# GpSimd adds the two tables' sums between the layers of a graph network, TensorE turns one sum

## The chip, the cores and the metric

The kernel runs on one core of a Trainium2 chip. The metric is the time of one execution in microseconds of the device. Engines are written as in the profile: PE is TensorE's matmul, PEld its weight load, DVE is VectorE, ACT is ScalarE, POOL is GpSimd, SP is SyncE, whose queue issues most transfers here.

## The reference

A graph of 6250 nodes with 256 features and 100000 edges, sorted by `dst`, goes through two layers. Layer 0 computes a message for each edge, sums the messages per node, and passes sum and node through a gated unit. Layer 1 is an attention over the edges with 8 heads. Each layer ends in a residual and a layer norm.

```python
msg = relu(concat[h[row], h[col], edge_attr] @ W1.T + b1) @ W2.T + b2
agg = segment_sum(msg, row, N)
gx = agg @ W_ih.T + b_ih                  # xr, xz, xn = split(gx)
gh = h @ W_hh.T + b_hh                    # hr, hz, hn = split(gh)
r, z = sigmoid(xr + hr), sigmoid(xz + hz)
n = tanh(xn + r * hn)
x1 = layernorm(h + (1 - z) * n + z * h)
# layer 1: s_u = x1 @ W_u.T + b_u, s_v = x1 @ W_v.T; softmax over the edges of a node,
# weighted sum of x1[src]; then layernorm(x1 + sum)
```

The kernel moves W2 behind the sum: layer 0 leaves for each node the sum of the 256 hidden values and a count of its edges, and the product of W2 and W_ih (`WcT`) is applied once per node.

## The kernel before

The program runs in phases with a barrier between them: setup, layer 0 over the edges (2/3 of the time), the nodes between the layers (`nodes_phase`), layer 1 over the edges, output. Nodes are dealt with in 49 blocks of 128 (a node in each partition).

Layer 0 adds its sums into two tables in memory, `S0` and `S1`, by turns. The sums of a node are therefore the sum of its rows in both. `nodes_phase` is the stage between the layers, and the only one that the change touches. A step of a block is a small function, and `pipeline(engine, stages)` writes each engine's order by hand: in round `j` an engine runs its steps in the order listed, each for the block that is so many blocks behind as the number beside it says. The first 7 rounds are written out, the rest is a loop with 7 rounds in its body. Steps of a block, in the order of the data:

- SP, `load` (L1318 to L1322): two transfers for `sums[:, 0, j]` and `sums[:, 1, j]`, one each for `hidden` (the products of W_hh) and `xs`. There are buffers for 7 blocks. In the loop a load stands behind `mixed` of the block that held the buffer, and behind the store of the block before that one (L1326), which waits for that block's last step.
- DVE `start` (L1438 to L1442): the count and the two `addend` operations.
- PE `turn_sums` (L1375): four matmuls against the identity, of 128x128 each, turn and add the two sums in PSUM (`psT`), two for each half of the 256 columns. ACT copies `psT` to `sumsT` (L1410).
- PE `gates` (L1385): four matmuls. DVE `keep_gates` (L1448, L1449), ACT sigmoid (L1414), DVE `candidate` (L1454, L1456), ACT tanh (L1418).
- POOL `mix` (L1352, L1353): `xs - cand` and `xs + cand`. DVE `update` (L1461 to L1468): three operations on the mixed values and the moments.
- POOL `deviation` (L1358 to L1363): root and shift of the norm from the moments. ACT normalises (L1424), PE turns `x1` (L1393) and computes the scores (L1400), DVE `finish` (L1473, L1474).

In a round POOL runs `deviation` three blocks behind and then `mix` two blocks behind. DVE runs `candidate` (2), `start` (0), `finish` (6), `keep_gates` (1), `update` (2). PE runs `gates` (1), `turn_sums` (0), `turn_x1` (4), `scores` (5). Each queue is strictly in this order, so POOL's `mix` of a block stands behind its `deviation` of the block before, and that one waits for DVE's `update` of the block before.

Of the kernel before, what the change touches and what calls it, by code (L numbers as in the profile page):

```python
# [7 lines left out]
ALU = mybir.AluOpType  # L8
# [3 lines left out]
P = 128  # L12
N, E, H, ED, NH = 6250, 100000, 256, 64, 8
# [13 lines left out]
NTAB = 2  # L27
# [31 lines left out]
def nth(i, j):  # L59

    return i * UNR + (j + 1)


def pipeline(engine, stages):

    def one_pass(i, first):
        for j in range(UNR):
            for behind, stage in stages:  # L70
                if j >= behind:
                    stage(i, j - behind)
                elif not first:
                    stage(i - 1, UNR + j - behind)

    one_pass(0, True)
    with engine.Fori(1, NI) as i:
        one_pass(i, False)
    for j in range(UNR, UNR + max(behind for behind, _ in stages)):
        for behind, stage in stages:  # L80
            if 0 <= j - behind < UNR:
                stage(NI - 1, j - behind)
# [1192 lines left out]
def nodes_phase(nc, K, D, A):  # L1275
# [3 lines left out]
    with ExitStack() as st:  # L1279
        m = Mem(nc, st, "nd_")  # L1280
        sums = m.sb("sums", [P, NTAB, UNR, UW])
# [15 lines left out]
        psT = m.ps("psT", [P, 512])  # L1297
# [3 lines left out]
        psS = m.ps("psS", [P, 512])  # L1301
        loaded = [m.sem(f"loaded{j}") for j in range(UNR)]
        stored = [m.sem(f"stored{j}") for j in range(UNR)]
        counted, sums_turned, sumsT_ready = m.sem("counted"), m.sem("sums_turned"), m.sem("sumsT_ready")
        gates_done, gates_kept, gates_open = m.sem("gates_done"), m.sem("gates_kept"), m.sem("gates_open")
        cand_ready, cand_done, mixed = m.sem("cand_ready"), m.sem("cand_done"), m.sem("mixed")
# [9 lines left out]
        @block.sync  # L1316
        def _(sp):
            def load(row, j, count=P):  # L1318
                for t in range(NTAB):
                    sp.dma_start(sums[:, t, j, :], D[f"S{t}"][bass.ds(row, P), :]).then_inc(loaded[j], 16)  # L1320
                sp.dma_start(hidden[:, j, :], D["GH"][bass.ds(row, P), :]).then_inc(loaded[j], 16)
                sp.dma_start(xs[0:count, j, :], A["x"][bass.ds(row, count), :]).then_inc(loaded[j], 16)  # L1322

            def store(i, j):
                sp.wait_ge(rows_ready, nth(i, j))
                sp.dma_start(D["X1"][bass.ds(i * (UNR * P) + j * P, P), :], x1[:, j, :]).then_inc(stored[j], 16)  # L1326

            for j in range(UNR):
                load(j * P, j)
            with sp.Fori(0, NI - 2) as i:  # L1330
                for j in range(UNR):

                    sp.wait_ge(mixed, i * (2 * UNR) + 2 * (j + 1))
                    sp.sem_inc(sp_waited, 1)
                    load(i * (UNR * P) + (UNR + j) * P, j)
                    store(i, j)
            for j in range(UNR):
                sp.wait_ge(mixed, (NI - 2) * 2 * UNR + 2 * (j + 1))
                row = (NI - 1) * UNR * P + j * P
                load(row, j, min(P, N - row))  # L1340
                store(NI - 2, j)
            for j in range(UNR):
                store(NI - 1, j)
            for j in range(UNR):
                sp.wait_ge(stored[j], 16 * NI)

        @block.gpsimd
        def _(pool):
            def mix(i, j):

                pool.wait_ge(cand_done, nth(i, j))
                nc.gpsimd.tensor_tensor(tmp[:, j, :], xs[:, j, :], cand[:, j, :], ALU.subtract).then_inc(mixed, 1)  # L1352
                nc.gpsimd.tensor_tensor(y[:, j, :], xs[:, j, :], cand[:, j, :], ALU.add).then_inc(mixed, 1)  # L1353

            def deviation(i, j):

                pool.wait_ge(moments_ready, nth(i, j))
                nc.gpsimd.tensor_tensor(rstd[:, j, :], moments[:, j, 1:2], K["eps"][:, :], ALU.add).then_inc(var_ready, 1)  # L1358
                pool.wait_ge(var_ready, i * (3 * UNR) + (3 * j + 1))
                nc.gpsimd.tensor_tensor(rstd[:, j, :], rstd[:, j, :], K["neghalf"][:, :], ALU.pow).then_inc(var_ready, 1)  # L1360
                nc.gpsimd.tensor_scalar(shift[:, j, :], moments[:, j, 0:1], -1.0, None, ALU.mult).then_inc(var_ready, 1)
                pool.wait_ge(var_ready, i * (3 * UNR) + (3 * j + 3))
                nc.gpsimd.tensor_tensor(shift[:, j, :], shift[:, j, :], rstd[:, j, :], ALU.mult).then_inc(rstd_ready, 1)  # L1363

            pipeline(pool, [(3, deviation), (2, mix)])

        @block.tensor
        def _(pe):
            def turn_sums(i, j):

                pe.wait_ge(sumsT_ready, i * UNR + j)
                pe.wait_ge(loaded[j], i * (16 * (NTAB + 2)) + 16 * (NTAB + 2))
                for k in range(HC):
                    for t in range(NTAB):
                        last = nc.tensor.matmul(psT[:, k * P:(k + 1) * P], sums[:, t, j, k * P:(k + 1) * P], K["ident"][:, :],  # L1375
                                                start=(t == 0), stop=(t == NTAB - 1))
                last.then_inc(sums_turned, 1)

            def gates(i, j):

                pe.wait_ge(gates_kept, i * UNR + max(j - 1, 0))
                pe.wait_ge(sumsT_ready, nth(i, j))
                for target, cols in ((psRZ[j % 2][:, :], slice(0, 2 * H)), (psN[j % 2][:, 0:H], slice(2 * H, 3 * H))):
                    for k in range(HC):
                        t = nc.tensor.matmul(target, sumsT[:, j, k * P:(k + 1) * P], K["WcT"][:, k, cols],  # L1385
                                             start=(k == 0), stop=(k == HC - 1))
                t.then_inc(gates_done, 1)

            def turn_x1(i, j):
                pe.wait_ge(x1T_ready, i * UNR + j)  # L1390
                pe.wait_ge(x1_ready, nth(i, j))
                for k in range(HC):
                    t = nc.tensor.transpose(psX[:, k * P:(k + 1) * P], x1[:, j, k * P:(k + 1) * P], K["ident"][:, :])  # L1393
                t.then_inc(x1_turned, 1)

            def scores(i, j):
                pe.wait_ge(rows_ready, i * UNR + j)
                pe.wait_ge(x1T_ready, nth(i, j))
                for k in range(HC):
                    t = nc.tensor.matmul(psS[:, 0:2 * NH], x1T[:, j, k * P:(k + 1) * P], K["WuvT"][:, k, :],  # L1400
                                         start=(k == 0), stop=(k == HC - 1))
                t.then_inc(scores_done, 1)

            pipeline(pe, [(1, gates), (0, turn_sums), (4, turn_x1), (5, scores)])

        @block.scalar
# [549 lines left out]
def build(nc, x, src, dst, edge_attr, W1, b1, W2, b2, W_ih, b_ih, W_hh, b_hh, W_u, b_u, W_v, out, stop=99):  # L1956
# [15 lines left out]
    with ExitStack() as st:  # L1972
# [19 lines left out]
        if stop < 2:  # L1992
            return
        nodes_phase(nc, K, D, A)
        inner.close()
        if stop < 3:
# [25 lines left out]
```

## Time and profile before

| | us |
|---|---|
| median of 3 runs | 4522.47 |
| lowest and highest | 4519.23, 4522.68 |
| the profiled execution, its own time | 4518.8 |
| its span, first to last instruction | 4517.1 |
| PE busy over the span | 3121.0 (69%) |
| DVE busy | 2158.0 (48%) |
| POOL busy | 3433.0 (76%) |
| ACT busy | 940.8 (21%) |
| first and last record of L1375 in the node phase | 2822.5, 3073.4 |

The node phase runs from about 2818 us to about 3089 us of the span, 6% of it. The shares over the whole span say nothing on it, so the rows further down are taken from its own window. A start in a row is counted from the span's beginning. The records of one engine may overlap by some hundredths of a microsecond, since an instruction's record begins while the one ahead of it ends.

### The profile page before, as it was taken

What the parts mean: (1) busy time and instruction counts of PE and PEld (TensorE: products, weight loads), DVE (VectorE), ACT (ScalarE), POOL (GpSimd) and SP (SyncE); (2) the same over time, 40 slices, a digit from 0 to 9 for tenths busy, and PEclk for the clock granted to TensorE, in tenths of its full rate; (3) what the DMA queues carried; (4) which work ended last, traced back from release to release, by engine and by line L of the source; (5) the groups of instructions that cost most, each with busy time, mean ns of one, the idle gap of its engine ahead of it and who ended that gap; (6) DMA issues with size and microseconds to landing.
All of it is one profiled execution on the core that took longest, in us unless ns stands there. A gap on an engine that the chain in (4) does not pass through costs nothing. (4 is left out here: it accounts for less than half of the span.)

```text
span 4517.1 us, 64322 instructions
## 1 busy us (share of the span) xinstructions
PE 3121.0 (69%) x13560; PEld 1920.1 (43%) x13561; DVE 2158.0 (48%) x4919; ACT 940.8 (21%) x2901; POOL 3433.0 (76%) x2886
## 2 busy tenths in 40 slices
PE   6688787787877878878788875884554554555552
PEld 3354444444444444444444443563433333333331
DVE  6433333333333333333333332886766666666767
ACT  2322222222222222222222221442000000000002
POOL 5568888888888888888888876566777777777775
PEclk8888888888888888888888888996776776776775
DMA  7787776777677767777777775555443344343342
GB/s 227 269 186 128 128 130 130 134 127 130 127 129 130 134 130 130 128 129 129 134 130 130 131 133 92 170 179 169 118 116 115 110 117 115 110 118 115 108 118 74
DMA packets 532854, 604.83 MB, mean 134 GB/s; under 512 B 170317, under 2 KB 451301, under 8 KB 532816
## 3 DMA queue, kind: packets, MB, share of 16 engines
q0 software_dynamic: 198144, 339.26, 39.2%
q1 hardware_dynamic: 319838, 242.37, 19.6%
q10 hardware_dynamic: 14834, 22.79, 1.5%
q8 instruction: 12, 0.20, 0.0%
q14 instruction: 26, 0.21, 0.0%
HBM read 435.31 MB, written 168.84 MB: 134 GB/s over the span
## 5 line engine op out<-in xcount | busy, mean ns | idle before, releaser
L1081 POOL DMA_INDIRECT S<-l_msum,l_sink x784 | 1278.3, 1631 | 279.0 <-issue 208.2
L1606 POOL DMA_INDIRECT l_feats<-X_rows,l_gsrc x880 | 1036.8, 1178 | 297.3 <-issue 258.7
L1064 POOL DMA_INDIRECT l_ga<-A_rows,l_gsrc x784 | 801.3, 1022 | 265.2 <-issue 158.9
L1154 PE MATMUL l_psU<-l_hid,l_same 128*128 128x257 f32 x1568 | 599.9, 469 | 489.7 <-ACT l_hid L1190 487.0
L1127 PE MATMUL l_psC<-l_table,l_onehot 128*128 x4728 | 741.3, 299 | 0.0
L1194 ACT COPY l_msum<-l_psU 128x257 f32<-128x257 f32 x784 | 292.6, 373 | 1877.4 <-POOLq L1080 1450.2
L1672 PE MATMUL l_psU<-l_feats,l_same 128*128 128x264 f32 x1760 | 537.6, 466 | 152.1 <-DVE l_feats L1841 135.2
L1120 PE MATMUL l_psC<-W1cT,l_attrT 64*128 64x256 f32 x1576 | 627.4, 482 | 12.9 <-DMA l_table<-B_rows 12.9
L1127 PEld LDWEIGHTS l_psC<-l_table,l_onehot 128*128 128x128 bf16 x4728 | 429.9, 105 | 373.8 <-issue 307.8
L1154 PEld LDWEIGHTS l_psU<-l_hid,l_same 128*128 128x128 f32 x1568 | 275.1, 220 | 618.3 <-ACT l_hid L1190 602.6
L1672 PEld LDWEIGHTS l_psU<-l_feats,l_same 128*128 128x128 f32 x1760 | 395.4, 233 | 287.5 <-issue 204.4
L1268 DVE TENSOR_TENSOR l_hidden<-l_psG,bgate 128x256 f32<-128x256 f32 x147 | 62.4, 425 | 864.7 <-PE l_psG L1169 864.7
L1120 PEld LDWEIGHTS l_psC<-W1cT,l_attrT 64*128 64x128 f32 x1576 | 264.1, 209 | 270.4 <-issue 237.9
L1226 DVE TENSOR_SCALAR l_togo<-srcT,spare 128x8 f32 x98 | 28.3, 289 | 699.2 <-POOLq L1080 699.2
L1190 ACT ACTIVATE l_hid<-l_ga 128x256 f32<-128x256 f32 x784 | 330.6, 422 | 0.0
L1243 DVE TENSOR_TENSOR l_ga<-l_ga,l_psC 128x256 f32<-128x256 f32 x784 | 308.4, 415 | 40.7 <-PE l_psC L1127 16.7
L1751 DVE TENSOR_TENSOR acc<-acc,l_psU 128x264 f32 x440 | 188.2, 428 | 226.8 <-PE l_psU L1672 194.4
L1841 DVE TENSOR_TENSOR l_feats<-l_feats 128x1024 f32<-128x1024 f32 x220 | 263.9, 1220 | 4.0 <-ACT l_feats L1704 0.4
L1169 PE MATMUL l_psG<-WhhT,l_xgT 128*128 128x256 f32 x588 | 210.8, 446 | 0.0
L1702 ACT ACTIVATE l_shrink<-l_psE 128x8 f32<-128x8 f32 x55 | 9.7, 177 | 954.6 <-PE l_psE L1659 954.6
L1217 DVE TENSOR_TENSOR l_same<-l_srcb,srcT 128x1024 f32<-128x1024 f32 x99 | 121.1, 1224 | 123.9 <-PE l_psU L1154 123.9
L1169 PEld LDWEIGHTS l_psG<-WhhT,l_xgT 128*128 128x128 f32 x588 | 136.8, 233 | 27.5
(357 smaller groups left out, 3264.9 us busy)
## 6 DMA issues: line engine op xcount, KB each, us to landing
l_srcb<-src_rows SPq DMA_DIRECT2D x396, 128.0 KB
l_locb<-lo_rows SPq DMA_DIRECT2D x55, 512.0 KB, 4.0
l_locb<-loc_rows SPq DMA_DIRECT2D x396, 64.0 KB
l_attr<-in_edge_attr SPq DMA_DIRECT2D x197, 128.0 KB, 3.5
GH_rows<-l_hidden SPq DMA_DIRECT2D x49, 384.0 KB
nd_hidden<-GH_rows SPq DMA_DIRECT2D x49, 384.0 KB, 3.1
l_feats<-X_rows,l_gsrc POOLq DMA_INDIRECT x880
S<-su_zeros ACTq DMA_DIRECT2D x12, 1156.5 KB
```

What stands on the lines that cost most here:

```text
L1064: pool.indirect_dma_start(ga[:, s, :], None, D["A"], bass.IndirectOffsetOnAxis(ap=gsrc[h][:, j % HALF:j % HALF + 1], axis=0)).then_inc(gat ...
L1081: pool.indirect_dma_start(D[f"S{j % NTAB}"], bass.IndirectOffsetOnAxis(ap=sink[j // HALF][:, j % HALF:j % HALF + 1], axis=0), msum[:, j % ...
L1120: nc.tensor.matmul(pc(j), attrT[j // 4 % 2][side, j % 4 // 2 * P:(j % 4 // 2 + 1) * P], K["W1cT"][side, :], start=True, stop=False)
L1127: t = nc.tensor.matmul(pc(j), onehot[j // HALF % 2][:, w, j % HALF, :], flat(table[:, bass.ds(blocks[j % 4] + w, 1), n * H:(n + 1) * H]), ...
L1154: nc.tensor.matmul(psU[j % 2][:, 0:UW], same[j // HALF][:, j % HALF, :], hid[:, j % RING, :], start=True, stop=True).then_inc(agg_done, 1)
L1169: t = nc.tensor.matmul(psG[:, 0:H], xgT[:, k * P:(k + 1) * P], K["WhhT"][:, k, n * H:(n + 1) * H], start=(k == 0), stop=(k == HC - 1))
L1190: nc.scalar.activation(hid[:, j % RING, 0:H], ga[:, j % SLOTS, :], ACT.Relu).then_inc(hid_ready, 1)
L1194: nc.scalar.copy(msum[:, j % RING, :], psU[j % 2][:, 0:UW]).then_inc(msum_ready, 1)
L1243: nc.vector.tensor_tensor(ga[:, s, :], ga[:, s, :], pc(j), ALU.add).then_inc(pre_ready, 1)
L1606: pool.indirect_dma_start(feats[r][:, t, :], None, D["X1"], bass.IndirectOffsetOnAxis(ap=gsrc[r][:, t:t + 1], axis=0)).then_inc(gathered[r ...
L1672: i = nc.tensor.matmul(psU[n % 4][:, 0:XW], same[:, t, :], feats[r][:, t, :], start=(t % PAIR == 0), stop=(t % PAIR == PAIR - 1))
L1841: nc.vector.tensor_tensor(f3, f3, w3, ALU.mult).then_inc(weighted, 1)
```

## The change

POOL gets a step `add_pair`: it waits for the block's four transfers and adds the second table's sums to the first's in place, over 256 columns. PE waits for this in place of the transfers, and turns the one sum with two transposes, where four matmuls stood. `add_pair` of the round's own block stands first in POOL's round, ahead of `deviation` and `mix`. The count (column 256) is still added on DVE. A new semaphore, `pair_added`, is taken ahead of those that follow it.

```diff
@@ nodes_phase
+        pair_added = m.sem("pair_added")
...
-            pipeline(pool, [(3, deviation), (2, mix)])
+            def add_pair(i, j):
+                pool.wait_ge(loaded[j], i * (16 * (NTAB + 2)) + 16 * (NTAB + 2))
+                nc.gpsimd.tensor_tensor(sums[:, 0, j, 0:H], sums[:, 0, j, 0:H], sums[:, 1, j, 0:H], ALU.add).then_inc(pair_added, 1)
+
+            pipeline(pool, [(0, add_pair), (3, deviation), (2, mix)])
...
             def turn_sums(i, j):
 
                 pe.wait_ge(sumsT_ready, i * UNR + j)
-                pe.wait_ge(loaded[j], i * (16 * (NTAB + 2)) + 16 * (NTAB + 2))
+                pe.wait_ge(pair_added, nth(i, j))
                 for k in range(HC):
-                    for t in range(NTAB):
-                        last = nc.tensor.matmul(psT[:, k * P:(k + 1) * P], sums[:, t, j, k * P:(k + 1) * P], K["ident"][:, :],
-                                                start=(t == 0), stop=(t == NTAB - 1))
+                    last = nc.tensor.transpose(psT[:, k * P:(k + 1) * P], sums[:, 0, j, k * P:(k + 1) * P], K["ident"][:, :])
                 last.then_inc(sums_turned, 1)
```

On POOL, in the body of the loop, this stands in a row before (the round's end and the next one; the names in brackets are those of semaphores, some of which carry the name that the same number had in the setup phase):

```order
L1352 TENSOR_TENSOR nd_tmp<-nd_xs,nd_cand 128x256 [waits nd_cand_done]
L1353 TENSOR_TENSOR nd_y<-nd_xs,nd_cand 128x256
L1358 TENSOR_TENSOR nd_rstd<-nd_moments,eps 128x1 [waits su_x_out]
L1359 REGISTER_ALU
L1360 TENSOR_TENSOR nd_rstd<-nd_rstd,neghalf 128x1 [waits su_x_keys_ready]
L1361 TENSOR_SCALAR nd_shift<-nd_moments 128x1
```

And with the change, where lines are moved by up to 7:

```order
L1353 TENSOR_TENSOR nd_tmp<-nd_xs,nd_cand 128x256 [waits nd_cand_done]
L1354 TENSOR_TENSOR nd_y<-nd_xs,nd_cand 128x256
L1368 TENSOR_TENSOR nd_sums<-nd_sums 128x256 [waits nd_loaded1]
L1359 TENSOR_TENSOR nd_rstd<-nd_moments,eps 128x1 [waits su_x_keys_ready]
L1360 REGISTER_ALU
L1361 TENSOR_TENSOR nd_rstd<-nd_rstd,neghalf 128x1 [waits su_x_mapped]
L1362 TENSOR_SCALAR nd_shift<-nd_moments 128x1
```

The add of the next round's block stands directly behind the second operation of `mix`, with no other instruction between them.

On PE, in the sixth of the rounds that are written out, before:

```order
L1375 MATMUL nd_psT<-ident,nd_sums 128x128 [waits nd_loaded5,nd_sumsT_ready]
L1375 MATMUL nd_psT<-ident,nd_sums 128x128 x3
L1393 MATMUL nd_psX<-ident,nd_x 128x128 [waits nd_x1_ready,nd_x1T_ready]
L1393 MATMUL nd_psX<-ident,nd_x 128x128
L1400 MATMUL nd_psS<-WuvT,nd_x1T 128x16 [waits nd_x1T_ready,nd_rows_ready]
L1400 MATMUL nd_psS<-WuvT,nd_x1T 128x16
```

And with the change, where the step has two instructions and waits for POOL:

```order
L1379 MATMUL nd_psT<-ident,nd_sums 128x128 [waits nd_pair_added,nd_sumsT_ready]
L1379 MATMUL nd_psT<-ident,nd_sums 128x128
L1396 MATMUL nd_psX<-ident,nd_x 128x128 [waits nd_x1_ready,nd_x1T_ready]
L1396 MATMUL nd_psX<-ident,nd_x 128x128
```

What stands around it on PE is as before.

## Rows read from the trace of the kernel before

**Rows 1.** Busy time in a stretch: length, PE, PEld, DVE, ACT, POOL, clock, DMA.

```profile
2900.00:2920.00 20.00, 17.71 (x89) 12.43 (x88) 17.38 (x52) 8.57 (x20) 12.78 (x24) 1.00 0.60 183
```

**Rows 2.** Waits of DVE and PE from 2867 to 3024: total us, times, longest.

```profile
DVE nd_tmp L1461 <- POOL nd_y L1353: 10.4, 29, 0.5
PE nd_psS L1400 <- DVE nd_x L1474: 19.9, 25, 1.1
```

**Rows 3.** Timeline, POOL and DVE in one round: start, us, engine, line, idle before.

```profile
2901.11 0.28 POOL L1358 TENSOR_TENSOR nd_rstd<-nd_moments,eps 128x1 f32<-128x1 f32 x1 [1.79 <-DVE nd_moments L1468]
...
2902.57 0.48 DVE L1442 SCALAR_TENSOR_TENSOR nd_addend<-b2ih,nd_count,bgate 128x256 f32<-128x256 f32 x1
...
2902.83 0.27 POOL L1363 TENSOR_TENSOR nd_shift<-nd_shift,nd_rstd 128x1 f32<-128x1 f32 x1
...
2903.06 0.73 POOL L1352 TENSOR_TENSOR nd_tmp<-nd_xs,nd_cand 128x256 f32<-128x256 f32 x1
...
2903.74 0.73 POOL L1353 TENSOR_TENSOR nd_y<-nd_xs,nd_cand 128x256 f32<-128x256 f32 x1
...
2904.50 0.42 DVE L1461 TENSOR_TENSOR nd_tmp<-nd_tmp,nd_rz 128x256 f32<-128x256 f32 x1 [0.37 <-POOL nd_y L1353]
...
2904.96 0.42 DVE L1463 TENSOR_TENSOR nd_y<-nd_y,nd_tmp 128x256 f32<-128x256 f32 x1
...
2905.42 0.43 DVE L1465 BATCH_NORM_STATS2 nd_stats<-nd_y 128x6 f32<-128x256 f32 x1
...
2905.99 0.18 DVE L1468 BATCH_NORM_AGGREGATE nd_moments<-nd_stats 128x2 f32<-128x6 f32 x1 [0.15 <-DVE nd_stats L1465]
...
2906.26 0.28 POOL L1358 TENSOR_TENSOR nd_rstd<-nd_moments,eps 128x1 f32<-128x1 f32 x1 [1.79 <-DVE nd_moments L1468]
```

**Rows 4.** Timeline, PE in one round, and SP's last load in the same round.

```profile
2903.72 1.96 PE L1385 MATMUL nd_psRZ<-WcT,nd_sumsT 128*128 128x512 f32 x4
...
2905.59 0.33 SPq L1322 DMA_DIRECT2D nd_xs<-in_x  x1
...
2906.39 1.05 PE L1375 MATMUL nd_psT<-ident,nd_sums 128*128 128x128 f32 x8
...
2907.28 0.38 PE L1393 MATMUL nd_psX<-ident,nd_x 128*128 128x128 f32 x2
...
2908.40 0.62 PE L1400 MATMUL nd_psS<-WuvT,nd_x1T 128*128 128x16 f32 x4 [0.74 <-DVE nd_x L1474]
```

**Rows 5.** Transfers into the `sums` buffers, from the view of that tile.

```profile
DMA to landing us min/median/max: 1.9/2.1/4.8
```

**Rows 6.** Timeline at the phase's start: DVE and POOL side by side.

```profile
2834.43 0.75 DVE L1440 SCALAR_TENSOR_TENSOR nd_addend<-b2ih,nd_count,nd_hidden 128x512 f32<-128x512 f32 x1
2834.86 0.91 POOL L1352 TENSOR_TENSOR nd_tmp<-nd_xs,nd_cand 128x256 f32<-128x256 f32 x1 [25.85 <-ACT nd_cand L1418]
2835.10 0.95 DVE L1442 SCALAR_TENSOR_TENSOR nd_addend<-b2ih,nd_count,bgate 128x256 f32<-128x256 f32 x1
...
2835.74 0.90 POOL L1353 TENSOR_TENSOR nd_y<-nd_xs,nd_cand 128x256 f32<-128x256 f32 x1
```

**Rows 7.** Timeline in the output phase: a large POOL add, a DVE operation on 3 columns.

```profile
4460.45 3.95 POOL L1904 TENSOR_TENSOR x_rows<-acc,x_rows 128x1792 f32<-128x1792 f32 x1
4461.06 3.36 DVE L1932 SCALAR_TENSOR_TENSOR ot_shift<-ot_moments,ot_rstd 128x3 f32<-128x3 f32 x1
```

**Rows 8.** Timeline at the phase's start: the first block on PE.

```profile
2822.50 2.04 PE L1375 MATMUL nd_psT<-ident,nd_sums 128*128 128x128 f32 x8 [30.48 <-DMA nd_xs<-in_x]
```

**Rows 9.** Stretches where the clock fell (columns as in Rows 1), and two rounds around them.

```profile
2970.20:2973.60 3.40, 2.27 (x7) 1.24 (x8) 2.96 (x10) 1.49 (x4) 1.81 (x3) 0.91 0.35 105
2973.60:2977.00 3.40, 3.40 (x13) 2.47 (x12) 2.69 (x9) 0.42 (x1) 3.04 (x6) 0.58 0.61 176
```

**Rows 10.** Timeline: POOL's first instruction of a round, two rounds apart.

```profile
2968.36 0.19 POOL L1358 TENSOR_TENSOR nd_rstd<-nd_moments,eps 128x1 f32<-128x1 f32 x1 [1.79 <-DVE nd_moments L1468]
...
2979.22 0.28 POOL L1358 TENSOR_TENSOR nd_rstd<-nd_moments,eps 128x1 f32<-128x1 f32 x1 [2.07 <-DVE nd_moments L1468]
```

## The prediction

> **What bounds the kernel now.** The change touches one phase of 6% of the span, so the page's shares of the whole are left aside and the phase's own window is read first [rows 1]. In 20 us PE is busy 17.7, DVE 17.4, POOL 12.8, at a granted clock of 1.00. Two engines near 87% could each be the bound, and the change takes work from one of them and gives work to the third. The list of waits decides between them [rows 2]: PE waits for DVE in nearly every block (19.9 us in 25 waits), DVE waits for POOL in nearly every block (10.4 us in 29). PE waits for nothing slower than itself only if it is not the bound, so PE has slack. The loop that sets the pace must run through POOL and DVE.
>
> The timeline of one round shows that loop [rows 3]. POOL starts `deviation` at 2901.11 when DVE's moments are there, is through with it at 3.10, mixes the next block until 4.47. DVE starts `update` 0.03 us later (4.50), having waited 0.37, and runs four operations up to the moments at 2905.99. These release POOL at 2906.26. The round takes 2906.26 - 2901.11 = 5.15 us, and all of it is this chain: 3.36 us of POOL, then some 1.7 us of DVE's `update`, then handovers. POOL's 1.79 us of idle time lies beside `update`. PE's round [rows 4] has its gates from 3.72, the turn at 6.39, the turn of `x1` at 7.28, and then it is idle for 0.74 us until DVE lets the scores go at 8.40.
>
> **What is removed.** The turn of the sums is 8 records of PE in 1.05 us; the two transposes of `x1` at L1393, which are the same form as the new ones, are 2 records in 0.38 us [rows 4]. So PE saves 0.67 us a block, 33 us over 49 blocks. In steady rounds this is worth nothing: the gates start behind the scores, and these wait for DVE. The saving becomes a longer wait there (0.74 becomes about 1.4). In the first block it counts: 8 records took 2.04 us there [rows 8], two would take a quarter, 0.5, with an add of 0.73 ahead. That is 0.8 us less, once.
>
> **What is added.** An add of 128x256 on POOL, the form of L1352 and L1353: 0.73 us each [rows 3]. By busy time it fits: it stands behind L1353, in 1.79 us of idle time, and POOL would be back 1 us before the moments come. Its wait is for transfers. The last one of a load is issued at 2905.59 [rows 4], lands 2.1 us later [rows 5] at 2907.7, and the add that needs it comes one round behind L1353's end, at 4.47 + 5.15 = 2909.6. So the wait is over 1.9 us before it is asked for, and `deviation` and `mix`, which queue behind it, aren't held. PE's new wait is over too: the add ends at 2910.3, PE turns that block at 6.39 + 5.15 = 2911.5.
>
> **Where the add costs.** The place is the trouble. It starts in the moment in which DVE's L1461 is released, and both read two tensors in SBUF. What the two engines do to each other there is seen at the phase's start [rows 6]. POOL's L1352 starts at 2834.86 inside DVE's L1440 and takes 0.91 in place of 0.73. DVE's L1442 is next in DVE's queue, and takes 0.95 in place of the 0.48 of [rows 3]; it ends at 2836.05, 0.28 us after POOL's record ended (2835.77). L1353 behind it takes 0.90. They don't share, they take turns, and the waiting one is served at the next change of instruction. The output phase shows the same with larger pieces [rows 7]: an operation of DVE on 3 columns takes 3.36 us and ends at 4464.42, with POOL's add at 4464.40. In the present rounds `mix` runs beside L1448 and L1449, which read PSUM and only one tensor of SBUF, and none of the four is longer for it; that is why POOL's work is free now.
>
> The price by order of arrival:
> - POOL first: L1353's successor starts at its end, 4.42 to 4.47, holds until about 4.42 + 0.73 = 5.15. L1461 ends 0.28 later, at 5.43, where it ended at 4.92. Cost 0.51 us a round.
> - DVE first: L1461 is through at 4.92, POOL goes next and needs 0.91 less the part it waited; from L1440's end (5.18) to L1352's end (5.77) in [rows 6] that is 0.59. It ends at 5.51, and L1463 0.28 later at 5.79, where it ended at 5.38. Cost 0.41 us.
> - The lower end is 0: DVE keeps its place through L1461 and L1463 and the add runs beside L1465, with one input. The upper end is the whole add, 0.73 us.
>
> A gain in this place is excluded, since nothing leaves the chain of POOL and DVE. I take 0.46, between the two orders. Everything behind L1461 in DVE's queue moves by it, the moments too, and so POOL's next round: nothing catches up, since POOL's own start hangs on those moments. An add follows a `mix` in 46 rounds (blocks 3 to 48), so 46 x 0.46 = 21.2 us. The bounds are 0 and 46 x 0.73 = 34 us.
>
> The Trainium skill ("SBUF — State Buffer", section "SBUF: two separate sides") says that GpSimd and a VectorE operation with two SBUF inputs take a shared pair of ports as an exclusive lock, the first one for its whole instruction. By its figure for the release, 115 ns after the holder's end, L1461 would begin at 5.27 and the estimate would be 0.77 us a round, 35 us; [rows 6] has the blocked operation ended 0.28 after the holder, so part of its time runs ahead, and the sum goes by that.
>
> **The clock.** PE's busy share goes from 17.7 of 20 to about (5.15 x 0.87 - 0.67) / 5.6 = 68%, with one gap of 1.4 + 0.5 us in each round. It has fallen here before [rows 9]: after a stretch in which PE was busy 2.27 of 3.4 us the granted clock was 0.91, then 0.58 while PE was busy throughout, which is a fall from 2.4 to 1.2 GHz. The two rounds around it took 2979.22 - 2968.36 = 10.86 us [rows 10] in place of 10.30, so a fall costs 0.56 us, most of it hidden by PE's slack. I take three more such falls, 1.7 us.
>
> The Trainium skill ("TensorE: Matmul & The Clock Gate", section "HAM oscillation — how this bites in real kernels") tells of kernels whose bursts of matmuls are so far apart that the clock falls in each pause. It speaks against a change that takes work from PE alone; that would be the third rival below.
>
> **The sum.** Against the profiled execution: 4518.8 + 21.2 - 0.8 + 1.7 = 4540.9. The median of the runs lies 3.7 above that execution, the lowest run 0.4; I add 2 and forecast **4543 us**, slower by 0.45%. A measurement of this kernel can tell some 0.2%, 9 us, from no change.
>
> **The rivals.**
> 1. *The add is hidden* (DVE keeps its place until L1465, or the two don't collide at this spot). For it: 1.79 us of idle time, and starts that lie within 0.1 us of each other. Against: [rows 6], where the waiting engine went next. The cost is then only the first block's gain and a fall or two: 4518.8 - 0.8 + 1 + 2 = 4521. Same.
> 2. *PE is the bound after all*, and its 0.67 us a block comes off: 49 x 0.67 = 33 us, 4490. Against it stand both rows of [rows 2]. Faster. That the two transposes would still be 8 records would give this no gain and the forecast the same time.
> 3. *The clock falls every second round.* The pause on PE is 1.9 us of 5.6, and the stretch that brought a fall had 1.1 us of idle time in 3.4. 23 falls x 0.56 = 13 us in place of 1.7: 4543 + 11 = 4554. It decides when a fall comes again after each recovery. Slower.
> 4. *The whole add or more lies on the chain* (or a late transfer holds POOL, with `deviation` and `mix` behind it): 46 x 0.73 = 34 us, 4556. Slower.
>
> **How the numbers follow.** The forecast has 0.58, rival 1 0.19, rival 2 0.03, rival 3 0.12, rival 4 0.08. Faster by over 0.2% is rival 2 and a little for what I don't see, 0.04. Within 0.2% is rival 1, with a share of the forecast where few rounds collide, 0.20. Slower is the rest, 0.76. The range takes in the forecast and rivals 1 and 3, and stops at rival 4's time: 4518 to 4557. The forecast's own range is 4536 to 4548 (0.41 and 0.51 a round, with two to eight falls).
>
> **What would show it.** In the changed profile: POOL's add at L1368 directly behind L1354 with about 0.73 us or more; L1461's operation (L1464 there) with 0.9 us in place of 0.42, or else the next one; the start-to-start time of POOL's L1359 at 5.6 in place of 5.15; PE's wait ahead of the scores near 1.9. If L1464 stays at 0.42 and the round at 5.15, rival 1 holds and my reading of [rows 6] fails for this place. If PE's wait for DVE vanishes, rival 2 does. If the granted clock in the phase is below 0.95 on the mean, rival 3.

## The result, and the profile after

| | before | with the change |
|---|---|---|
| median of 6 runs | 4522.18 | 4542.50 |
| lowest and highest | 4518.44, 4525.91 | 4534.63, 4544.14 |
| the profiled execution | 4518.8 | 4544.14 |
| its span | 4517.1 | 4542.4 |

The ratio is 1.0039, with a 95% interval of 1.0028 to 1.0049. The change makes the kernel slower by 20 us. The forecast was 4543.

The waits in the middle of the node phase, 2870 to 3030 us, answer to [rows 2] (total us, times, longest):

```profile
DVE nd_tmp L1464 <- POOL nd_y L1354: 9.4, 27, 0.4
PE nd_psS L1403 <- DVE nd_x L1477: 36.6, 26, 2.3
```

DVE waits for POOL's `mix` as it did (0.35 us each time), and PE waits for DVE for 1.41 us in place of 0.80. So PE's saving went into waiting. The timeline of one round answers to [rows 3]: start, us, engine, line, with the idle time before in brackets.

```profile
2921.69 0.73 POOL L1353 TENSOR_TENSOR nd_tmp<-nd_xs,nd_cand 128x256 f32<-128x256 f32 x1
...
2922.38 0.72 POOL L1354 TENSOR_TENSOR nd_y<-nd_xs,nd_cand 128x256 f32<-128x256 f32 x1
...
2923.07 0.72 POOL L1368 TENSOR_TENSOR nd_sums<-nd_sums 128x256 f32<-128x256 f32 x1
2923.14 0.93 DVE L1464 TENSOR_TENSOR nd_tmp<-nd_tmp,nd_rz 128x256 f32<-128x256 f32 x1 [0.38 <-POOL nd_y L1354]
...
2924.11 0.42 DVE L1466 TENSOR_TENSOR nd_y<-nd_y,nd_tmp 128x256 f32<-128x256 f32 x1
...
2924.57 0.43 DVE L1468 BATCH_NORM_STATS2 nd_stats<-nd_y 128x6 f32<-128x256 f32 x1
...
2925.14 0.18 DVE L1471 BATCH_NORM_AGGREGATE nd_moments<-nd_stats 128x2 f32<-128x6 f32 x1 [0.15 <-DVE nd_stats L1468]
...
2925.41 0.28 POOL L1359 TENSOR_TENSOR nd_rstd<-nd_moments,eps 128x1 f32<-128x1 f32 x1 [1.62 <-DVE nd_moments L1471]
```

POOL's add starts 0.07 us ahead of DVE's L1464 and takes its plain 0.72 us. L1464 takes 0.93 in place of 0.42, and ends 0.28 us behind the add (2924.07 against 2923.79). The round that ended with this row began at 2919.75: 5.66 us, where it was 5.15. POOL still idles 1.62 us in it. From the views of the tiles, over all 49 blocks: the count, then the durations (min/median/max) in ns, then the first and the last start in us:

```profile
L1368 POOL TENSOR_TENSOR nd_sums<-nd_sums x49: 714/722/989, 2825.1 to 3094.4; 128x256 f32<-128x256 f32 x49
L1464 DVE TENSOR_TENSOR nd_tmp<-nd_tmp,nd_rz x49: 417/932/942, 2838.0 to 3109.5; 128x256 f32<-128x256 f32 x49
L1466 DVE TENSOR_TENSOR nd_y<-nd_y,nd_tmp x49: 424/425/832, 2838.7 to 3110.0; 128x256 f32<-128x256 f32 x49
```

The other order of arrival occurred as well, in the last block that has an add. The add was later by 0.09 us than elsewhere (a gap of 0.06 behind `mix` where the records overlap otherwise), DVE got in first, and the next operation paid:

```profile
3094.33 0.43 DVE L1464 TENSOR_TENSOR nd_tmp<-nd_tmp,nd_rz 128x256 f32<-128x256 f32 x1 [0.37 <-POOL nd_y L1354]
3094.79 0.83 DVE L1466 TENSOR_TENSOR nd_y<-nd_y,nd_tmp 128x256 f32<-128x256 f32 x1
```

```profile
3094.35 0.99 POOL L1368 TENSOR_TENSOR nd_sums<-nd_sums 128x256 f32<-128x256 f32 x1
```

That round took 5.56, 0.41 more than 5.15. Of the 46 adds that follow a `mix`, 42 made L1464 0.93 or 0.94 us long and two made it 0.68 and 0.70. One was DVE first, as shown. The last one, at 2991.56, met nothing: PE's gates were late, DVE waited for them, and the add was over before L1464 began.

```profile
2991.42 0.69 DVE L1451 TENSOR_TENSOR nd_rz<-nd_psRZ,nd_addend 128x512 f32<-128x512 f32 x1 [1.08 <-PE nd_psN L1388]
...
2991.56 0.73 POOL L1368 TENSOR_TENSOR nd_sums<-nd_sums 128x256 f32<-128x256 f32 x1
...
2992.36 0.42 DVE L1464 TENSOR_TENSOR nd_tmp<-nd_tmp,nd_rz 128x256 f32<-128x256 f32 x1
```

That round took 5.86.

**The account.** The first start of POOL's `deviation` and the last lie 248.65 us apart before (2838.64 to 3087.29) and 271.26 after (2840.01 to 3111.27): 22.6 us more in 48 rounds. The stretch from DVE's first operation of the phase to the first `deviation` is 1.30 us shorter (16.25 before, 14.95 after). The two profiled executions differ by 25.3; the other 4.0 lie ahead of the phase (2.7) and behind it (1.3), where the programs are the same.

### The profile page after: what moved, and what is told of

It reads as the page before. It is cut to its first block and busy times, and to the rows that moved or that the text cites. A ratio compares the mean times of both kernels' runs of the same rounds, so it can differ in the third digit from the quotient of the medians.

```text
span 4542.4 us, 63789 instructions
## 1 busy us (share of the span) xinstructions
PE 3125.2 (69%) x13266; PEld 1903.9 (42%) x13267; DVE 2182.0 (48%) x4919; ACT 939.1 (21%) x2901; POOL 3468.8 (76%) x2935
```

## The experiments

"The round" is the median distance between two starts of POOL's first `deviation` instruction, read from the timeline of each kernel. "The 48 rounds" is the distance from the first to the last of these starts. Each kernel is timed beside the kernel before, on the same chip. Not all experiments were on one chip, so the ratios are to be compared rather than the times. My theory was that the add and DVE's operation exclude each other. The rivals were that POOL's queue became too long, that PE's lower clock costs something, and that PE was the bound.

### turn_only: the gain without the add

This kernel leaves the second table's sums out of its result. Its edit, against the change (`add_pair` and its semaphore go too):

```diff
-                pe.wait_ge(pair_added, nth(i, j))
+                pe.wait_ge(loaded[j], i * (16 * (NTAB + 2)) + 16 * (NTAB + 2))
...
-            pipeline(pool, [(0, add_pair), (3, deviation), (2, mix)])
+            pipeline(pool, [(3, deviation), (2, mix)])
```

> The change without its add: PE turns only the first table's sums with two transposes and waits for the transfers as before; POOL is as before. The second table's sums are left out of the result. If the loop of POOL and DVE sets the pace (my theory), the round stays at 5.15 us, PE waits about 1.4 us or more for DVE ahead of the scores, and the time is that of before less some 1 us for the first block. If PE were the bound (rival), the round is 4.5 to 4.9 us and the time 4490 to 4510. If the fallen clock of PE costs something by itself (rival), the round is above 5.2 on the mean and the time above 4526.

The round is 5.15, the 48 rounds 248.91 us. The ratio is 0.9989 (0.9980 to 0.9999), medians 4524.19 and 4525.85. PE waits for DVE:

```profile
PE nd_psS L1398 <- DVE nd_x L1472: 36.3, 27, 1.7
```

That is 1.34 us each time. PE was not the bound: its busy time in 100 us fell from 86.4 to 76.3 us, and the phase's rounds stayed as they were. These are the kernel before and, below it, turn_only: length, then busy us (and instructions) of PE, PEld, DVE, ACT, POOL, then the granted clock, DMA share and GB/s.

```profile
2860.00:2960.00 100.00, 86.39 (x433) 61.27 (x431) 86.76 (x252) 43.27 (x97) 62.63 (x117) 1.00 0.58 179
```

```profile
2860.00:2960.00 100.00, 76.27 (x304) 47.87 (x304) 86.53 (x252) 41.49 (x96) 62.28 (x116) 0.95 0.57 173
```

The mean clock from 2860 to 3060 was 0.95 in place of 0.99, and the 48 rounds are 0.26 us longer than before. The saving did show in the first rounds, where the queues are still filling: from DVE's first operation to the first `deviation` there are 13.44 us, where it was 16.25.

### add_only: the add without the gain

Against the kernel before:

```diff
+        scratch = m.sb("scratch", [P, UNR, 512])
...
+            def add_pair(i, j):
+                pool.wait_ge(loaded[j], i * (16 * (NTAB + 2)) + 16 * (NTAB + 2))
+                nc.gpsimd.tensor_tensor(scratch[:, j, 0:H], sums[:, 0, j, 0:H], sums[:, 1, j, 0:H], ALU.add).then_inc(pair_added, 1)
+
+            pipeline(pool, [(0, add_pair), (3, deviation), (2, mix)])
```

> The change without its gain: POOL adds the two sums at the same place, with the same wait, into a buffer of its own that nobody reads; PE has its four matmuls and waits for the transfers as before. If the collision of POOL's add with DVE's first operation of update is the cause, the round is 5.66 us as with the change, DVE's L1461 takes 0.93 us and the time is 22 to 25 us above before. If the fallen clock of PE has a part in the loss (rival), the clock is back near 1.00 here and the round is shorter than 5.66.

The round is 5.66, the 48 rounds 271.03 us, against 271.26 with the whole change. The ratio is 1.0051 (1.0034 to 1.0068), medians 4551.74 and 4525.85: 25.9 us, just above the 22 to 25 that were expected. The add alone carries the whole loss. It also bounds what the clock costs. These two stretches are add_only and, below it, the change, with the columns as above.

```profile
2845.00:3115.00 270.00, 212.86 (x1013) 148.63 (x1011) 234.28 (x608) 102.54 (x236) 184.97 (x333) 0.96 0.47 144
```

```profile
2840.00:3110.00 270.00, 203.48 (x738) 124.94 (x738) 233.47 (x608) 103.31 (x236) 185.60 (x333) 0.88 0.46 144
```

A mean clock of 0.88 in place of 0.96 goes with 0.23 us more in the 48 rounds. PE has less work in the change as well, so this is the clock and the saving together. (The clock was expected to come back near 1.00 here.)

### fill: POOL is busy in the same place, but reads nothing

As add_only, with its buffer `scratch`, but with another step:

```diff
+            def add_pair(i, j):
+                nc.gpsimd.memset(scratch[:, j, :], 0.0).then_inc(pair_added, 1)
```

> In place of the add POOL fills a buffer of its own with zeros, 512 columns, some 0.5 us, directly behind the second operation of mix; it reads nothing from SBUF and waits for nothing. PE is as before. If POOL's reading of SBUF is what blocks DVE, the round stays at 5.15 us and L1461 at 0.42. If any work of POOL in that place holds DVE or POOL's own next step (rival), L1461 takes 0.6 to 0.75 and the round 5.3 to 5.5.

```profile
2926.70 0.52 POOL L1368 MEMSET nd_scratch<- 128x512 f32 x1
```

```profile
2926.79 0.43 DVE L1466 TENSOR_TENSOR nd_tmp<-nd_tmp,nd_rz 128x256 f32<-128x256 f32 x1 [0.37 <-POOL nd_y L1355]
```

POOL works 0.5 us at the very spot, and DVE's operation takes its 0.43 (0.43 at most over all 49 blocks). The round is 5.15, the 48 rounds 248.88, the ratio 0.9996 (0.9986 to 1.0006). It is not POOL's time that costs, and not the release of DVE by a busy POOL. The fill is shorter than the add (0.52 against 0.72), but the next experiment has an add of 0.46 that does cost. Fill and adds differ in what POOL reads from SBUF. A POOL instruction that reads a single tensor was not tried in this place.

### add_128 and add_512: the size of the add

The first added line is add_128's, the second add_512's; both are add_only otherwise, and the lines are shown without their semaphore.

```diff
-nc.gpsimd.tensor_tensor(scratch[:, j, 0:H], sums[:, 0, j, 0:H], sums[:, 1, j, 0:H], ALU.add)
+nc.gpsimd.tensor_tensor(scratch[:, j, 0:P], sums[:, 0, j, 0:P], sums[:, 1, j, 0:P], ALU.add)
...
+nc.gpsimd.tensor_tensor(scratch[:, j, 0:2 * H], hidden[:, j, 0:2 * H], hidden[:, j, H:3 * H], ALU.add)
```

> As add_only (an add into a buffer that nobody reads, PE as before), but over 128 columns. An add of 256 takes 0.72 us and a memset of 512 0.52, so the add of 128 should take some 0.4 us, and with POOL first DVE's L1461 ends 0.28 us after POOL's record: about 0.2 us later than before. If the price is the time for which POOL holds, the round is 5.30 to 5.40 us. If a collision has a fixed price (rival), it is 5.66.

> As add_only, but POOL adds 512 columns of two parts of the hidden products, some 1.3 us, also into a buffer that nobody reads. By the held time the round is 5.15 + 0.51 + 0.6 = 6.2 to 6.35 us and L1461 takes about 1.5 us; POOL's own idle time (1.79 us) would hide it all if the lengths of the queues counted. By a fixed price (rival) the round is 5.66.

DVE's operation in the two (views of the tile; ns):

```profile
L1467 DVE TENSOR_TENSOR nd_tmp<-nd_tmp,nd_rz x49: 425/661/669, 2844.4 to 3102.9; 128x256 f32<-128x256 f32 x49
```

```profile
L1467 DVE TENSOR_TENSOR nd_tmp<-nd_tmp,nd_rz x49: 425/1475/1481, 2845.0 to 3141.3; 128x256 f32<-128x256 f32 x49
```

| columns | POOL's record | DVE's operation | round | more than 5.15 |
|---|---|---|---|---|
| none | | 0.42 | 5.15 | |
| 128 | 0.46 | 0.66 | 5.39 | 0.24 |
| 256 | 0.72 | 0.93 | 5.66 | 0.51 |
| 512 | 1.27 | 1.48 | 6.20 | 1.05 |

The price is POOL's record less 0.21 or 0.22 us, at each size. A fixed price for a collision is out. So is the length of the queue: with 512 columns POOL had 0.5 us to spare in the round of before, and the round still grew by 1.05. Both rounds are as expected for a price by the time held. One execution each was timed, 4537.32 and 4577.32, beside a median of 4525.43.

### add_late: the whole change, the add moved by a wait

Against the change:

```diff
             def add_pair(i, j):
                 pool.wait_ge(loaded[j], i * (16 * (NTAB + 2)) + 16 * (NTAB + 2))
+                if not isinstance(i, int) or j >= 3:
+                    pool.wait_ge(y_ready, i * UNR + (j - 2))
```

> The whole change, but POOL's add also waits until DVE's second operation of update (y) is done, so that it runs beside the statistics, which have one input. If the collision with L1464 is the cause, L1464 and L1466 are back at 0.42 us each. The add then starts 0.9 us later and ends some 0.1 to 0.2 us into DVE's next operation with two inputs (L1457), so the round is 5.15 to 5.35 us and the time 0 to 10 us above before. If the cause is the length of POOL's queue (rival), the added wait makes it worse: the round is 5.8 or more.

```profile
2928.96 0.42 DVE L1466 TENSOR_TENSOR nd_tmp<-nd_tmp,nd_rz 128x256 f32<-128x256 f32 x1 [0.37 <-POOL nd_y L1354]
2929.42 0.43 DVE L1468 TENSOR_TENSOR nd_y<-nd_y,nd_tmp 128x256 f32<-128x256 f32 x1
2929.89 0.43 DVE L1470 BATCH_NORM_STATS2 nd_stats<-nd_y 128x6 f32<-128x256 f32 x1
2930.00 0.73 POOL L1370 TENSOR_TENSOR nd_sums<-nd_sums 128x256 f32<-128x256 f32 x1 [1.06 <-DVE nd_y L1468]
```

The add now begins with the statistics. The round is 5.20, the 48 rounds 250.48, the ratio 1.0002 (0.9993 to 1.0012). One more wait, which holds POOL back for 1.06 us, takes 0.46 of the 0.51 us away. The add's end still touches the next operation with two inputs (L1459, 0.44 in place of 0.39).

### add_on_dve: the same add on DVE

Against the change, with POOL's `add_pair` taken out:

```diff
                 nc.vector.tensor_tensor(count[:, j:j + 1], sums[:, 0, j, H:UW], sums[:, 1, j, H:UW], ALU.add).then_inc(counted, 1)
+                nc.vector.tensor_tensor(sums[:, 0, j, 0:H], sums[:, 0, j, 0:H], sums[:, 1, j, 0:H], ALU.add).then_inc(pair_added, 1)
```

> The change with its add on DVE in place of POOL: behind the count in start, 0.42 us; POOL's queue is that of before. By the naive account DVE has 0.37 us of waiting in each round to give, and the round is 5.15 to 5.25, the time 4520 to 4530. My theory of the shared reading: the add moves L1440 and L1442 by 0.35 to 0.42 us, POOL's L1361, L1363 and then L1352 wait behind them, mix ends as much later, and the round is 5.5 to 5.6, the time 16 to 21 us above before.

The round is 5.36, the ratio 1.0019 (1.0010 to 1.0029). Both accounts missed: 5.15 to 5.25 was too little and 5.5 to 5.6 too much. The rows show why.

```profile
2917.24 0.15 DVE L1437 TENSOR_TENSOR nd_count<-nd_sums 128x1 f32<-128x1 f32 x1
2917.31 0.42 DVE L1438 TENSOR_TENSOR nd_sums<-nd_sums 128x256 f32<-128x256 f32 x1
...
2917.65 0.74 DVE L1440 SCALAR_TENSOR_TENSOR nd_addend<-b2ih,nd_count,nd_hidden 128x512 f32<-128x512 f32 x1
2917.74 0.74 POOL L1362 TENSOR_SCALAR nd_shift<-nd_moments 128x1 f32<-128x1 f32 x1
```

From the count to L1440 there are 0.41 us; in before the same distance is 0.19, since L1440 waits for the count. So the add moves what follows by 0.22 only. These 0.22 come in full: POOL's one-column operation on the shift takes 0.74 beside L1440 in place of 0.53, and `mix` is later by it, and DVE waits for `mix` as long as before (8.6 us in 23 waits, 0.37 each). DVE's waiting time was not free to use, because what it waits for was moved along. Two rounds took 6.67 us: the clock had fallen there, and DVE waited 1.7 us for PE's gates.

### mix_first: the chain cut, no add

Against the kernel before:

```diff
-            pipeline(pool, [(3, deviation), (2, mix)])
+            pipeline(pool, [(2, mix), (3, deviation)])
...
-            pipeline(act, [(2, bound), (0, keep_sums), (3, normalise), (1, open_gates), (4, keep_x1)])
+            pipeline(act, [(2, bound), (0, keep_sums), (1, open_gates), (3, normalise), (4, keep_x1)])
```

> The kernel before with POOL's round in the other order, mix and then deviation, and ACT's sigmoid ahead of its normalisation; no add, PE as before. The chain of moments, deviation, mix, update is cut. If that chain sets the pace, the round falls to what DVE needs, 4.8 to 5.1 us, with mix now beside L1440 and L1442 (some 0.4 us of waiting for each other): the time is 3 to 15 us below before. If DVE's own work was the bound (rival), the collision makes it 5.2 to 5.6 us.

The round is 5.16, the ratio 1.0001 (0.9992 to 1.0011). DVE no longer waits for POOL at all, but `mix` now lies beside the addend operations:

```profile
2923.57 0.92 POOL L1352 TENSOR_TENSOR nd_tmp<-nd_xs,nd_cand 128x256 f32<-128x256 f32 x1 [2.04 <-ACT nd_cand L1418]
2923.81 0.95 DVE L1442 SCALAR_TENSOR_TENSOR nd_addend<-b2ih,nd_count,bgate 128x256 f32<-128x256 f32 x1
```

What the cut chain gave (0.37 us of waiting) is about what the collision takes (0.95 against 0.48); the next experiment tests that. My time range was missed; the rival's (5.2 to 5.6) too, just.

### spread: both, and the version that is faster

On top of mix_first:

```diff
+            def start_rest(i, j):
                 nc.vector.scalar_tensor_tensor(addend[:, j, 2 * H:3 * H], K["b2ih"][:, 2 * H:3 * H], count[:, j:j + 1],
...
+            def gather_moments(i, j):
                 dve.wait_ge(stats_ready, nth(i, j))
...
-            pipeline(dve, [(2, candidate), (0, start), (6, finish), (1, keep_gates), (2, update)])
+            pipeline(dve, [(2, candidate), (0, start), (1, keep_gates), (6, finish), (2, update), (0, start_rest), (2, gather_moments)])
```

> The kernel before (no add, PE as before) with mix_first's orders on POOL and ACT, and DVE's order changed so that its operations on PSUM (L1448, L1449 of before) and the small ones of finish run beside POOL's mix, and the second addend operation stands between the statistics and the aggregate, where DVE waits 0.15 us in each round. If the two engines' shared reading is what mix_first still paid (0.47 us on that addend operation), the round is 4.75 to 4.95 us, and the time 10 to 18 us below before. If something else holds the round at 5.15 (rival: DVE's own work, or PE's gates, which now have 1.3 us less), it is 5.0 to 5.2 and the time within 5 us of before.

The round is 4.76, the 48 rounds 227.60 us. The ratio is 0.9946 (0.9925 to 0.9967), medians 4590.30 and 4609.65. The round is as expected, the gain of 19.4 us a little over the 10 to 18. This run and spread_change were on one chip, spread_again and spread_add_ahead on another; the kernel before took 4610 and 4602 us on them, so only the ratios are compared. Repeated as spread_again, beside the last experiment:

> The kernel of spread once more, beside spread_add_ahead on one chip: the round is 4.76 us and the time 15 to 22 us below before (48 rounds of 5.15 to 4.76, 19 us).

The round is 4.76 again, the 48 rounds 227.48, the ratio 0.9954 (0.9930 to 0.9978). In spread's own rows, with `mix` beside the operations on PSUM, nobody is long:

```profile
2994.22 0.41 DVE L1450 TENSOR_TENSOR nd_cand<-nd_psN,nd_addend 128x256 f32<-128x256 f32 x1
2994.25 0.73 POOL L1353 TENSOR_TENSOR nd_y<-nd_xs,nd_cand 128x256 f32<-128x256 f32 x1
...
2996.28 0.47 DVE L1443 SCALAR_TENSOR_TENSOR nd_addend<-b2ih,nd_count,bgate 128x256 f32<-128x256 f32 x1
```

### spread_change and spread_add_ahead: the change on those orders

The first added line is the order of spread_change, the second that of spread_add_ahead; ACT and DVE have the orders of spread.

```diff
-            pipeline(pool, [(0, add_pair), (3, deviation), (2, mix)])
+            pipeline(pool, [(2, mix), (3, deviation), (0, add_pair)])
+            pipeline(pool, [(0, add_pair), (2, mix), (3, deviation)])
```

> The whole change on the orders of spread, with POOL's add at the end of its round, behind deviation. By my theory the add costs only what it overlaps of DVE's operations with two SBUF inputs, and that is the update or the addend operation at the round's end: 0 to 0.5 us a round above spread. If PE is near its bound in spread's shorter round, the change's 0.67 us of PE could give some of it back (rival): then this round is the shorter of the two.

spread_change was much slower than either account: 1.0157 (1.0111 to 1.0203), the rounds 6.5 to 7.9 us. PE stood waiting for POOL's add:

```profile
PE nd_psT L1379 <- POOL nd_sums L1368: 52.2, 22, 3.6
DVE nd_rz L1452 <- PE nd_psN L1388: 27.3, 19, 3.4
```

I had put the add of the round's own block behind `mix` and `deviation` of that round. So the turn waited for the sum of a round that itself waited for the turn. The last experiment moves it one round ahead, where the change has it:

> As spread_change, with POOL's add where the change has it, first in its round, so directly behind the deviation of the round before: it is a round earlier than in spread_change, and PE should not wait for it any more. It then starts as DVE comes to its second addend operation, which should take 0.95 to 1.05 us in place of 0.47. By the theory of the held reading the round is 4.76 + 0.5 = 5.2 to 5.3 us and the time 0 to 6 us above before. If PE's queue was what made spread_change slow (rival to the late add), the round stays above 6.

```profile
2992.22 1.03 DVE L1446 SCALAR_TENSOR_TENSOR nd_addend<-b2ih,nd_count,bgate 128x256 f32<-128x256 f32 x1
2992.23 0.73 POOL L1368 TENSOR_TENSOR nd_sums<-nd_sums 128x256 f32<-128x256 f32 x1
```

The round is 5.30, 0.54 above spread, and the operation that meets the add takes 1.03 in place of 0.47, both as expected. The ratio to before is 0.9998 (0.9977 to 1.0018). The change costs the same half microsecond on a kernel with other orders, and it meets another operation of DVE there.

## Why the prediction was right

- **The bound.** The reading of [rows 2] and [rows 3] holds: turn_only shows that PE's 0.67 us a block are worth nothing in the steady rounds (its round is that of before), and PE's wait for DVE rose from 0.80 to 1.41 us.
- **The place of the price.** L1464 was named, with 0.9 us in place of 0.42, and a round of 5.6; it took 0.93, and the round is 5.66. The reason, two instructions that read SBUF and take turns, is borne out by add_only (the add alone does it), fill (a POOL instruction that reads nothing does not), and the row of three sizes.
- **Its size.** 0.51 was worked out for POOL first, 0.41 for DVE first. Both occurred, with these very numbers: POOL first in full in 42 of 46 rounds, DVE first in one. The 0.46 that was taken between them was too low by 0.05, or 2 us: the records told who comes first (4.42 to 4.47 against 4.50), and I should have gone by them. The 48 rounds grew by 22.6 us, against 21.2. The estimate by the figure of the Trainium skill's page "SBUF — State Buffer" ("SBUF: two separate sides"), 0.77, was too high. That figure is told there of GpSimd waiting for VectorE; here VectorE waits, and its operation of 0.42 ended 0.28 after POOL's record. The page's rule of exclusion agrees with the runs, also in that an instruction of POOL which reads nothing doesn't take part.
- **The first block.** 0.8 us less was expected. From DVE's first operation to the first gates of PE there are 2.71 us before (2822.39 to 2825.10) and 2.14 with the change (2825.06 to 2827.20): 0.57 less. The two transposes took 0.66 in place of the 0.5 of the forecast. The 1.30 us of the account above take in the next rounds too; the same stretch is 16.25, 16.87 and 17.25 us in before, fill and add_only, where PE's work is the same, so 1.3 is hardly more than this scatter.
- **The clock.** This term was wrong, though small. The clock did fall far oftener than the three more times I took: seventeen times from 2838 to 3110 (read in windows of 1 us), against three before, to 0.88 on the mean. The busy share of 68% was worked out with DVE's 0.87; with PE's 17.7 of 20 it is 69%. The price of 0.56 a fall was misread from [rows 10]: of the two long rounds there, 0.3 us is the turn of the 7-round loop, which every seventh round has, also where the clock was at 1.00 (3041.32 to 3046.77 is 5.45). The other 0.27 is the fall's, since DVE waited for the slow gates:

```profile
2976.54 0.69 DVE L1448 TENSOR_TENSOR nd_rz<-nd_psRZ,nd_addend 128x512 f32<-128x512 f32 x1 [0.64 <-PE nd_psN L1385]
```

  With the change there are two such waits, 0.61 at 2865.50 and 1.08 at 2991.42. The second by itself made that round 0.71 longer than 5.15; since the add met nothing there, the round is 0.20 above 5.66. All falls together come to 0.23 us beside add_only. So rival 3's fact came true almost without its price: a fall costs where PE's gates come too late for DVE, and PE's longer wait kept most of them in time.
- **The waits added.** Neither shows up. POOL goes from `mix` into the add without a gap, and PE's wait for POOL is not among its waits in the steady rounds.
- **The total.** 20.3 us between the medians, 25.3 between the profiled executions. The 4.0 us of the latter that lie outside the phase were not in the sum, and belong to no part of the change. The mechanism and its 0.41 to 0.51 us a round are what the experiments bear out. That the forecast of 4543 lies within 1 us of the median of 4542.50 is partly luck: the rounds were put 1.4 us too low and the clock 1.5 too high, the 2 us for the distance of profile and median were a guess, and the six executions with the change spread over 9.5 us. The forecast's own range is not what its terms give at the lower end: 4518.8 + 46 x 0.41 - 0.8 + 1.1 + 2 = 4540, not 4536.

## What to carry to other kernels

When a second engine idles beside a chain, look at what the chain's engine reads during that idle time, not only at how long it is: an elementwise operation with two inputs, moved to GpSimd, cost its own length less 0.2 us where VectorE reads two tensors in SBUF, and next to nothing where VectorE reads PSUM and one tensor (as `mix` does beside L1448 and L1449) or one tensor alone (add_late: 0.05 us a round). Where the idle time begins with the release of the other engine, the two start together, and here they collided in all but one of 46 rounds. Take work from an engine only when the waits say that others wait for it, and if a round is set by a chain over two engines, put the order of both queues right first (here 0.5% of the time, against 0.1% from less matmul work in turn_only).

## What was not expected of the hardware

- A collision costs the holder's record less 0.21 us, whatever the size: 0.24, 0.51, 1.05 us for adds of 128, 256 and 512 columns, which take 0.46, 0.72 and 1.27 us.
- With TensorE at a mean granted clock of 0.88, 48 rounds were 0.23 us longer than at 0.96 (add_only), in 271 us, where TensorE had 1.4 us of waiting in each round of 5.66. In add_on_dve, two falls made a round 1.3 us longer each (6.67 against 5.36).
- An added operation of 0.42 us moved DVE's queue by 0.22 (add_on_dve), since the next one had been waiting for the one ahead of it.
